# Turning the bf16 rests of three tiles in seven by transposing DMAs in a 16-head cross-attention stage

## What is computed

```python
HEADS = 16; DIM_HEAD = 64; SCALE = DIM_HEAD ** (-0.5); MASK_NEG = 1000000.0
kv = context @ Wkv
k, v = jnp.split(kv, 2, axis=-1)
q = x @ Wq
q, k, v = (_split_heads(q), _split_heads(k), _split_heads(v))
dots = jnp.einsum('bhnd,bhmd->bhnm', q, k) * SCALE
dots = dots - (1.0 - mask.astype(jnp.float32))[:, None, :, None] * MASK_NEG
attn = jax.nn.softmax(dots, axis=-1)
out = jnp.einsum('bhnm,bhmd->bhnd', attn, v)
out = out.transpose(0, 2, 1, 3).reshape(b, n, h * d)
return out @ Wout + bout
```

## Time and profile before

| | before |
|---|---|
| median of 3 runs | 3592.65 us (3586.34 to 3593.73) |
| the profiled execution, its own time | 3594.13 us |
| span of the profiled execution | 3592.4 us |
| PE busy, over the whole span | 3089.1 us, 86% |
| first and last start of the rest's transposes (L1571) | 607.1 and 1798.2 us |
| transposes of the rest on PE (L1571) | 2688, of 219 ns each |
| copies of them by ACT (L1631) | 224, of 1438 ns each |
| transposing DMAs of the high parts (L1499) | 224 |

### The profile page before, as it was taken

One profiled execution on the slowest core, in us unless ns is written; L12 is line 12 of the kernel. 1 busy time (PEld: TensorE's weight loads), 2 busy tenths in 40 slices (PEclk: granted clock), 3 DMA queues, 4 the chain that ended last, 5 costly groups with the idle time before them and its releaser, 6 DMA issues. The chain is left out here.

```text
span 3592.4 us, 75092 instructions
## 1 busy us (share of the span) xinstructions
PE 3089.1 (86%) x30284; PEld 2146.4 (60%) x30284; DVE 2302.8 (64%) x4272; ACT 1744.5 (49%) x2862; POOL 1864.5 (52%) x1046
## 2 busy tenths in 40 slices
PE   5977995999999999999959996799999983419959
PEld 3654544777777777777738775355555542216634
DVE  3546554777777777777634444699899865633445
ACT  2534332666665666656624543366666651104535
POOL 0003544777777777777632110488788770005316
PEclk9988996999999999999979997699999995559979
DMA  5740005766767666766514663343333310054500
GB/s 96 143 123 1 1 1 108 144 139 132 146 129 139 139 132 138 141 135 141 96 41 179 241 238 148 89 102 94 91 101 91 95 37 6 0 86 87 103 29 11
DMA packets 607381, 367.71 MB, mean 102 GB/s; under 512 B 462933, under 2 KB 566626, under 8 KB 606786
## 3 DMA queue, kind: packets, MB, share of 16 engines
q1 hardware_dynamic: 607042, 362.96, 43.7%
HBM read 174.41 MB, written 75.24 MB: 69 GB/s over the span
## 5 line engine op out<-in xcount | busy, mean ns | idle before, releaser
L1674 POOL TENSOR_TENSOR L_plo<-L_p,L_phi 128x1500 bf16<-128x1500 f32 x224 | 659.1, 2942 | 291.2 <-DVE L_phi L1750 289.8
L1631 ACT COPY L_ptlo<-L_lt 128x1536 bf16<-128x1536 bf16 x224 | 322.1, 1438 | 406.3 <-PE L_lt L1571 406.3
L2020 ACT ACTIVATE L2b_p<-L2b_score 125x448 f32<-125x448 f32 x768 | 378.7, 541 | 276.8 <-PE L2b_score L1933 274.2
L1585 PE MATMUL L_acc<-L_chi,L_pthi 125*128 125x128 bf16 x2688 | 462.1, 219 | 0.0
L1587 PE MATMUL L_acc<-L_chi,L_ptlo 125*128 125x128 bf16 x2688 | 461.4, 219 | 0.0
L1586 PE MATMUL L_acc<-L_clo,L_pthi 125*128 125x128 bf16 x2688 | 461.2, 219 | 0.0
L1739 DVE TENSOR_SCALAR_CACHE_REDUCE L_p<-L_score,L_cols 128x1500 f32<-128x1500 f32 x224 | 395.3, 1765 | 83.0 <-PE L_score L1563 82.8
L1750 DVE CAST L_phi<-L_p 128x1500 bf16<-128x1500 f32 x224 | 297.5, 1328 | 164.1 <-ACT L_p L1625 163.2
L1625 ACT ACTIVATE L_p<-L_p,L_least 128x1500 f32<-128x1500 f32 x224 | 346.5, 1547 | 67.4 <-DVE L_p L1739 63.3
L2063 POOL TENSOR_TENSOR L2b_psum<-L2b_p 125x896 f32<-125x896 f32 x128 | 266.9, 2085 | 134.6 <-ACT L2b_p L2020 132.2
L2091 DVE TENSOR_REDUCE L2b_max<-L2b_m 112x1 f32<-112x1000 f32 x256 | 300.4, 1194 | 26.6 <-PE L2b_m L1914 18.8
(11 more groups left out here) (632 smaller groups left out, 6917.5 us busy)
## 6 DMA issues: line engine op xcount, KB each, us to landing
L2b_kst<-L_keys SPq DMA_DIRECT2D x96, 375.0 KB, 5.6
L_ct<-L_ct SPq DMA_DIRECT2D x32, 768.0 KB, 5.7
L2a_ct<-L_ct SPq DMA_DIRECT2D x32, 768.0 KB, 14.3
L_ctx<-dram_ctx SPq DMA_DIRECT2D x32, 750.0 KB
L_keys<-L2a_kout SPq DMA_DIRECT2D x32, 750.0 KB, 7.6
L_values<-L2a_vout SPq DMA_DIRECT2D x32, 750.0 KB
L2b_vin<-L_values SPq DMA_DIRECT2D x32, 750.0 KB
L0x_ctx<-dram_ctx SPq DMA_DIRECT2D x32, 672.0 KB
```

The costliest lines, as they stand in the source:

```text
L1585: pe.matmul(acc, w_hi[0:KP, t, :], v_hi[0:KP, t, :], start=(t == 0), stop=False)
L1631: act.copy(pt_lo[g % 2][:, :, :], lt_ps[:, 0:KT * 128].rearrange("p (t q) -> p t q", t=KT)).then_inc(lo_read, 1)
L1674: pool.tensor_tensor(p_lo[g % 2][:, :, 0:KP], probs[g % RP][:, :].rearrange("q (t k) -> q t k", t=KT), p_hi[g % 2][:, :, 0:KP], ALU.subtra ...
L2020: act.activation(probs[t % RP][:, half * 2 * GW:(half + 1) * 2 * GW], score_ps[half][0:KP, 0:2 * GW], ACT.Exp).then_inc(exp_done, 1)
```

## The change

In tiles 2, 4 and 6 of each batch (`BY_DMA`), 96 of 224, the rest `p_lo` is no longer turned by PE and copied by ACT. SP issues a transposing DMA from `p_lo` straight into `pt_lo` (`turn_rest`), behind `turn_probs` of the same tile. `weighted` of such a tile waits for that DMA, and so does POOL's `rest` two tiles on, which writes the same `p_lo`.

```diff
+    BY_DMA = (2, 4, 6)
...
+                def turn_rest(g):
+                    sp.wait_ge(lo_ready, g + 1)
+                    wait(sp, av_done, g - 1)
+                    sp.dma_start_transpose(pt_lo[g % 2][:, :, :], p_lo[g % 2][:, :, :].rearrange("p t k -> p (t k)")
+                                           ).then_inc(lo_moved, 16)
...
                         turn_probs(QT * b + r)
+                        if r in BY_DMA:
+                            turn_rest(QT * b + r)
...
                 def turned(g):
 
+                    if by_dma(g):
+                        return
                     pe.wait_ge(lo_ready, g + 1)
-                    wait(pe, lo_read, g)
+                    wait(pe, lo_read, passed(g) - 1)
...
                     pe.wait_ge(*is_turned(g))
-                    pe.wait_ge(lo_read, g + 1)
+                    if by_dma(g):
+                        pe.wait_ge(lo_moved, 16 * moved(g))
+                    else:
+                        pe.wait_ge(lo_read, passed(g))
...
                 def read(g):
-                    act.wait_ge(lo_turned, g + 1)
+                    if by_dma(g):
+                        return
+                    act.wait_ge(lo_turned, passed(g))
...
                 def rest(g):
                     pool.wait_ge(hi_ready, g + 1)
-                    wait(pool, lo_turned, g - 1)
+                    if g >= 2 and by_dma(g - 2):
+                        pool.wait_ge(lo_moved, 16 * moved(g - 2))
+                    elif g >= 2:
+                        pool.wait_ge(lo_turned, passed(g - 2))
```

More of the change, by code:

```diff
@@ L1453, in heads_attention @@
         hi_ready, lo_ready = sem("hi_ready"), sem("lo_ready")
+        lo_moved = sem("lo_moved")
         hi_turned, lo_turned, lo_read = [sem(f"hi_turned{i}") for i in range(RT)], sem("lo_turned"), sem("lo_read")
@@ L1467, in is_turned, with by_dma, moved, passed @@
             return hi_turned[g % RT], 16 * (g // RT + 1)
+        def by_dma(g):
+            return g % QT in BY_DMA
+        def moved(g):
+            return sum(1 for x in range(g + 1) if by_dma(x))
+        def passed(g):
+            return g + 1 - moved(g)
         def tile(g):
```

## The result

| | before | after |
|---|---|---|
| median | 3593.19 us (3585.91 to 3596.61, 8 runs) | 3601.47 us (3600.60 to 3610.77, 8 runs) |
| the profiled execution, its own time | 3594.13 us | 3600.6 us |
| span of it | 3592.4 us | 3598.9 us |

The ratio is 1.0031, with a 95% interval of 1.0020 to 1.0042: the kernel became slower, by 8 to 11 us. I had forecast 3589 us and no change, with this outcome at 27%.

What follows compares the result with a forecast made beforehand. DVE, ACT and POOL were taken to lead most tiles, PE only a few. -7.0 (14 pairs) - 1.8 (last pair) + 3.0 (late landings) + 2.0 (start) = -3.8 us, giving 3589 us; range 3570 to 3612 us.

Steps and rivals of the forecast that it cites:

- the second rival: At the end of every second batch, transposing DMAs delay tile 1's high part: 20 us slower, 3613 us; chance 28%.
- What PE's time is worth: Transposes taken from PE gain 0.5 us a pair (0.39 at tile 6, 0.11 at tile 9), 7.0 us in 14 pairs.
- "Finish" holds back what tiles 2 and 4 give: The "finish" unit waits for DVE's L1707 before tile 6, so PE's earlier time from tiles 2 and 4 gains 0.
- The full gain: Rival: PE bounds the stage at 98%, so all its time is gained: 64 us, 3529 us; chance 5%.
- the partial one: Rival: "finish" starts 1 us earlier and tile 9 counts, 1.7 us a pair, 24 us, 3567 us; chance 15%.
- The last pair and the end: Half of at most 4.0 us gained in the last pair, 0.2 off for the last tile's DMA: 1.8 us.
- The start: Landings that take still longer, once or twice: 2 us added, between 0 and 5.
- The DMA share: In a pair of the changed kernel, the DMA engines' share rises from 0.68 to about 0.85.
- POOL's piece hides a landing up to 8.6 us: POOL's context piece holds up tile 3's cast anyway, so tile 1's high part landing at 1064.7 is free.
- Most pairs should be like the second, so I take 0.2 us for each of 15 such places: Late landings of tile 1's high part behind the context's load, every second batch: 3 us lost in all.
- The bound of 1.5 us a place: Upper limit of the loss at each of the 15 late landings of tile 1's high part, 22 us in all.

Runs made afterwards that it cites:

- e1: Changed kernel with the rests of tiles 2, 4 and 6 of a batch not turned at all, by PE or DMA: 3585.48 us, 0.9978 of before.
- e3: Changed kernel with the context's load split into 112 and 13 partitions: 3590.41 us, 0.9997 of before.
- e5: Changed kernel with only tiles 2 and 4 of a batch by DMA, tile 6 back on PE: 3590.26 us, 0.9993 of before.
- e4: Kernel before with the context's load split into 112 and 13 partitions: 3591.64 us, 0.9997 of before.
- e2: Kernel before with 96 more transposing DMAs at the same places, into a spare tile nobody reads: 3595.16 us, 1.0009 of before.
- e6: Changed kernel with 50 idle PE waits per DMA tile, restoring the 1788 PE instructions of a pair: 3594.25 us, 1.0004 of before.
- e8: Changed kernel with the load split into 112 and 13 partitions and only tiles 6, 7 and 8 of each pair by DMA: 3585.16 us, 0.9971 of before.
- e7: Changed kernel with the unsplit context load issued behind tile 2 of the batch before the one where it stood: 3637.51 us, 1.0119 of before.

## Why the prediction was wrong

The direction was wrong. The place was that of the second rival, the late landing of tile 1's high part, at 12.4 us for its 27. Its reason, each DMA slower in each of 15 places, was not: six of 14 pairs lost 0.3 us or less.

- **What PE's time is worth: right.** Forecast 0.5 us a pair, from tiles 6 and 9; measured 0.42 (75.42 to 75.00), in e1 and e3 without a disturbance and in five pairs of the changed kernel. e5 confirms the division among tiles. Over 14 pairs that is -5.9 us for the forecast -7.0.
- **"Finish" holds back what tiles 2 and 4 give: right.** It waits for L1738 14 times in 14 pairs, longer than before. The full gain and the partial one (3529 and 3567 us) fell with this row, and with e1's 8 us for all.
- **The last pair and the end: too favourable.** The last pair gave 2.0 us, but the stretch to the last product grew by 1.7 (17.3 to 19.0), where I had taken 1.0 for the last tile and counted half of the rest: -0.3 us for the forecast -1.8. e1, which turns no rest there, takes 14.6, so the last rest's DMA costs up to 4.4 us on the path.
- **The start: right.** +1.8 us for +2.0, and it is a late landing: tile 8's high part of the first pair, issued behind a load at 643.15, landed after 10.9 us, and tile 10's cast stood for it. In e3 it landed after 6.0 and this stretch is 59.7 us. The size is in part luck, since the stretch takes 61.5 us in e1 and 62.1 in e4 too, for another reason, in the first three tiles.

```profile
654.09 0.94 DVE L1781 CAST L_phi<-L_p 128x1500 bf16<-128x1500 f32 x1 [2.36 <-issue]
```

- **The DMA share: above the forecast.** 0.93 over the pairs and not 0.85; without the waits behind the load, in e3, 0.88.
- **POOL's piece hides a landing up to 8.6 us: right.** The good pair above shows it: the cast starts late and ends 0.80 us after the piece all the same. The Trainium skill, "SBUF — State Buffer", on the shared port pair, has the later engine fully blocked and not slowed. The traces agree, with a cast of 0.98 us in the kernel after, started 0.18 us before the piece's end, and one of 1.78 us in the kernel before, started 0.98 us before it, both ending 0.80 us after it.
- **"Most pairs should be like the second, so I take 0.2 us for each of 15 such places": this step failed.** It was +12.4 us in 14 pairs and not +3, by the 1062.5 us of the changed kernel against the 1050.1 of e3. The basis was good: the load goes out late, and tile 1's high part lands at 8.5 to 8.8 in six of 14 pairs, where I had 8.5 to 9.3. Where the packets keep their places the term itself is right: 2.4 us in 14 pairs in e2 and in e6. But I let the burst meet nothing but itself, and took it that pairs alike before would be alike after. Eight times in 14 it met more than that, and with a packet of code in it or ahead of it, landed at 9.3 to 11.6. The bound of 1.5 us a place was passed twice (2.0 and 3.05 us).

By the table, +1.8 + 6.6 - 2.0 + 1.7 makes 8.1 us. The medians lie 8.3 us apart and the two profiled executions 6.5; that it comes out so near the medians is luck, given how the rest of the program varies.

What I could have seen: the page of the kernel before has 241 instruction packets in its own row, 7.0 to a pair, and each pair was like the next. The change takes 150 PE instructions from a pair, 0.6 of a packet. An edit to the count of a pair by an amount that isn't a whole number of packets ends that regularity. As a statement of the size of a packet the Trainium skill, "Runtime: NRT & Kernel Launch", on the mechanics of instruction fetch, has refills of 16 KiB or 256 instructions, and calls the cost of crossing a boundary mostly hidden. The row of the queue agrees on the size (3.80 MB in 232 packets), and the 12 pairs from the second on agree on the count, 255 of PE's instructions a packet both before and after. In e1, with the same 232 packets, every pair takes 75.0 us, so PE doesn't pay for them; in the changed kernel it is another transfer, at the tightest place of the DMA engines, that pays.

What stays open: why the last mark comes 1.5 us late by a packet of 1.0 us, and why not each time. A packet that began 9.57 us after the load's issue did no harm and one at 9.68 did; the profile doesn't say which DMA engine a packet was on. Nor is it shown by an experiment that the packets ahead of the load, and those of q14, are what makes the other marks late: they stand in just the six pairs where these came at 9.1 us or later, and in e2 and e6, where no q8 packet runs ahead of the load, only the three pairs with q14's have landings of 9.1 to 9.3.

## What to carry to other kernels

Count what a moved operation costs on the path it goes to at the place where that path is already full, not at its average share: here the 64 of tiles 2 and 4 cost nothing (e5), and with the 32 of tile 6 the load went out late and the DMA behind it paid. Where a stage repeats with a steady period, ask what keeps time with it that is not in the program, the code packets above all (count the instructions of a period against 256), and don't carry a margin of half a microsecond from two sampled pairs to all of them. Then put the edit only where a gain gets through to the end of the chain: 48 tiles moved at the right places gave more than 96, both with the load split (1047.6 us in e8, 1050.1 in e3).

## What the runs showed of the hardware

- A load to 125 partitions of SBUF, at a DMA share of 0.30, holds a transposing DMA behind it, 5.9 to 6.9 us from issue to landing in the kernel before; in 112 and 13 partitions it does not (3.6 to 4.9 us in e4). In the changed kernel the longest landing is 11.6 us, and 7.7 with the split.
- Code comes in packets of 16 KB by the same DMA engines, most of them 0.9 to 1.4 us long in the stage, and 256 PE instructions to a packet by the counts above (1788 and 1638 in a pair, 7.0 and 6.4 packets). One of them can make the last of a transposing DMA's 16 marks 1.5 us late (43 of 200 that had one close before their end). In e7 two such packets took 5.9 and 6.4 us themselves.
- The clock of TensorE fell after the longest of these waits. In the pair of 78.05 us `weighted` waited 2.8 us for its high part, and windows of 2 us show this (the length, then PE, PEld, DVE, ACT and POOL busy, the granted clock, DMA share and GB/s):

```profile
1448.00:1450.00 2.00, 0.24 (x3) 0.24 (x4) 0.21 (x1) 0.00 (x0) 0.44 (x1) 0.89 1.69 356
1450.00:1452.00 2.00, 2.00 (x22) 2.00 (x20) 2.00 (x3) 0.00 (x0) 1.18 (x1) 0.50 0.60 130
1452.00:1454.00 2.00, 2.00 (x23) 2.00 (x22) 1.24 (x5) 1.47 (x2) 2.00 (x2) 0.76 1.25 274
```

PE was busy for 0.24 us of the 2 us from 1448, and the granted clock was 0.50, its lower level of 1.2 GHz, for 3.4 us from 1449.6 before it was back at 1.00. In the other pairs the mean clock is 1.00. It cost nothing more here: the pair is 3.05 us longer than the good ones, and its landing was 3.05 us later than the 8.6 that are free.
